# Running sums and new weights of an attention loop, moved from GpSimd to VectorE

## The reference

```python
xn = layernorm(x, g_in)
q = (xn @ Wq).reshape(b, n, H, DH).transpose(0, 2, 1, 3) * scale
kv = xn @ Wkv                       # one key and one value for all heads
sim = einsum('bhid,bjd->bhij', q, k) + bias          # k and v begin with the null key
sim = where(causal or hidden, -max, sim)
attn = softmax(sim, axis=-1)
out = layernorm((attn @ v).reshape(b, n, INNER) @ Wo, g_out)
# second part
xn = out / rms(out) * norm_weight
logits = xn @ router_weight.T + router_bias          # the top 512 tokens of each expert are chosen
y = fc2(gelu(fc1(xn[idx])))                          # 16 experts, 512 -> 2048 -> 512
x = x + (sum of y * gates) / (sum of gates)
```

## Time and profile before

| | |
|---|---|
| median of 3 runs | 2039.32 us (2038.94 to 2042.92) |
| the profiled execution | 2042.92 us, span 2041.2 us |
| busy, share of the span | PE 91%, VectorE (DVE) 75%, ScalarE (ACT) 65%, GpSimd (POOL) 59% |
| granted TensorE clock, mean | 0.961 of full speed |

### The profile page before, as it was taken

The page is one execution under the profiler, slowest core; times in us unless marked ns, Lnnn a source line. Parts: engine busy times, 40 slices in busy tenths (PEclk is TensorE's granted clock), DMA queues, the critical chain, the costliest instruction groups (busy, mean ns, idle before and its releaser), DMA issues.

```text
span 2041.2 us, 41281 instructions
## 1 busy us (share of the span) xinstructions
PE 1861.3 (91%) x12276; PEld 1654.0 (81%) x12276; DVE 1531.3 (75%) x2360; ACT 1321.4 (65%) x2624; POOL 1210.5 (59%) x1224
## 2 busy tenths in 40 slices
PE   2789999986159999999999999999999999999996
PEld 1678888875148898988999889888988999998895
DVE  5678899974886778787777777777777777777763
ACT  3667777762735766666676666666666676766663
POOL 1568888865035646575665657565665756656551
PEclk9899999997559999999999999999999999999998
DMA  5775444432923344353533435254343525434351
GB/s 191 239 207 170 114 120 117 126 98 70 345 63 112 109 133 114 118 139 103 139 108 124 120 123 139 93 142 110 119 124 118 142 90 149 107 125 133 99 130 31
DMA packets 96108, 263.09 MB, mean 129 GB/s; under 512 B 20433, under 2 KB 22193, under 8 KB 93105
## 3 DMA queue, kind: packets, MB, share of 16 engines
q1 hardware_dynamic: 79026, 228.21, 35.1%
q0 software_dynamic: 17024, 34.19, 9.0%
HBM read 223.47 MB, written 55.60 MB: 137 GB/s over the span
## 4 chain that ended last, share of the span: by engine, by line
PE 65%; DVE 4%; ACT 2%; issue 1%; POOL 1%; DMA 0%; DVEq 0%; ACTq 0%; POOLq 0%
PE experts_b_a L2185 17%; PE experts_b_y L273 11%; PE experts_b_y L272 11%; PE experts_b_y L274 11%; PE experts_b_b L2185 9%; PE experts_b_c L2185 4%; ACT experts_h L1697 2%; PE experts_b_turn L2165 1%; DVE experts_x_lo L1851 1%; PE experts_b_turn L2174 1%; PE experts_b_c L2174 1%; DVE experts_w_lo L1911 0%; POOL experts_rows L1521 0%; DVE experts_h_lo L1914 0%; POOL experts_rows_meta L1508 0%
## 5 line engine op out<-in xcount | busy, mean ns | idle before, releaser
L272 PE MATMUL experts_b_y<-experts_w_hi,experts_h_hi 128*128 128x512 f32 x1024 | 406.5, 397 | 0.0
L273 PE MATMUL experts_b_y<-experts_w_lo,experts_h_hi 128*128 128x512 f32 x1024 | 404.6, 395 | 0.0
L274 PE MATMUL experts_b_y<-experts_w_hi,experts_h_lo 128*128 128x512 f32 x1024 | 399.6, 390 | 0.0
L1483 POOL TENSOR_TENSOR experts_s_raw<-experts_w_raw 128x256 f32<-128x256 f32 x128 | 131.9, 1031 | 432.2 <-DMA experts_w_raw<-in_w 431.3
L2185 PE MATMUL experts_b_a<-experts_x_hi,experts_w_hi 128*128 (+1 forms) x1024 | 290.6, 284 | 7.3 <-ACT experts_u_copy L1665 3.2
L2185 PE MATMUL experts_b_a<-experts_x_hi,experts_w_lo 128*128 (+1 forms) x1024 | 290.4, 284 | 0.0
L2185 PE MATMUL experts_b_a<-experts_x_lo,experts_w_hi 128*128 (+1 forms) x1024 | 290.3, 284 | 0.0
L274 PEld LDWEIGHTS experts_b_y<-experts_w_hi,experts_h_lo 128*128 128x128 f32 x1024 | 192.6, 188 | 43.3
L2185 PEld LDWEIGHTS experts_b_a<-experts_x_hi,experts_w_hi 128*128 128x128 f32 x1024 | 195.2, 191 | 27.6 <-issue 6.3
L272 PEld LDWEIGHTS experts_b_y<-experts_w_hi,experts_h_hi 128*128 128x128 f32 x1024 | 194.5, 190 | 24.1
L273 PEld LDWEIGHTS experts_b_y<-experts_w_lo,experts_h_hi 128*128 128x128 f32 x1024 | 194.5, 190 | 21.2
(11 more groups left out here) (366 smaller groups left out, 5489.0 us busy)
## 6 DMA issues: line engine op xcount, KB each, us to landing
experts_w_raw<-in_w SPq DMA_DIRECT2D x256, 512.0 KB
attend_bias<-in_bias SPq DMA_DIRECT2D x68, 256.0 KB, 4.1
attend_spread_w<-weight_dram SPq DMA_DIRECT2D x34, 512.0 KB, 6.5
xn_dram<-g_out_row SPq DMA_DIRECT2D x6, 2304.0 KB, 9.4
attend_q_x<-in_x SPq DMA_DIRECT2D x17, 256.0 KB, 2.9
attend_k_x<-in_x SPq DMA_DIRECT2D x17, 256.0 KB, 5.8
xn_dram<-attend_xn SPq DMA_DIRECT2D x17, 256.0 KB, 4.4
experts_b_sb<-in_b SPq DMA_DIRECT2D x16, 256.0 KB
```

The source lines that it names most:

```text
L272: nc.tensor.matmul(out, lh, rh, start=first, stop=False)
L273: nc.tensor.matmul(out, lh, rl, start=False, stop=False)
L274: return nc.tensor.matmul(out, ll, rh, start=False, stop=last)
L1483: nc.gpsimd.tensor_tensor(s1, a21, a22, ALU.add).then_inc(s_done, 1)
```

## The change

Three operations on 128x16 numbers go from GpSimd to VectorE, and the reciprocal that stood between them joins them in one function `new_sums`. On VectorE the function stands after `key_stats` and before `key_parts`, where before only the reciprocal stood, between `value_parts` and the second `scale_new`. The read of `carry` goes with it. The read of the row number for `keep_logits` moves from ahead of `out_stats` to just ahead of the operation that uses it. Two waits that guarded the hand-over between the engines fall away or change engine.

```diff
--- before.py
+++ after.py
@@ -569,25 +569,6 @@
                     nc.gpsimd.tensor_tensor(state[:, 1, g, :], spread_w[:, 0, g, :], spread_w[:, 1, g, :],
                                             ALU.add).then_inc(o_ready[b], 1)
 
-                def new_sums(n, carry):
-                    done(pool, alpha_ready, n)
-                    free(pool, weight_ready, n)
-                    free(pool, sum_ready, n)
-                    nc.gpsimd.tensor_tensor(kept_sum[:, :], alpha[:, :], flat(total[:, bass.ds(carry, 1), :]), ALU.mult)\
-                        .then_inc(sum_kept, 1)
-                    for c in range(NG):
-                        done(pool, probs_ready[c], n)
-                    free(pool, inv_ready, n)
-                    done(pool, sum_kept, n)
-                    nc.gpsimd.tensor_tensor(total[:, 1, :], kept_sum[:, :], sums[:, :], ALU.add).then_inc(sum_ready, 1)
-
-                def new_weight(n):
-                    new = weight[:, :, :, :].rearrange("p t w g -> p w g t")
-                    done(pool, inv_ready, n)
-                    free(pool, weight_turned, n)
-                    nc.gpsimd.tensor_tensor(new[:, 0, :, :], kept_sum[:, :].rearrange("p (g t) -> p g t", t=2),
-                                            new[:, 1, :, :], ALU.mult).then_inc(weight_ready, 1)
-
                 pool.wait_ge(begun, 1 + CONSTANTS)
 
                 def turn(j, on, upto, edge):
@@ -613,16 +594,10 @@
                         mask_bias(j - 2, 0)
                     if on(-6):
                         out_root(j - 6)
-                    if on(-3):
-                        carry = number(pool, j - 3, 6, 1)
                     if on(0):
                         query_root(j)
-                    if on(-3):
-                        new_sums(j - 3, carry)
                     if on(-6):
                         gain(j - 6)
-                    if on(-3):
-                        new_weight(j - 3)
                     if on(-4):
                         scale_old(j - 4, 0)
                     if on(-2):
@@ -873,12 +848,25 @@
                     g = slice(c * GH, (c + 1) * GH)
                     rest(n, flat(pT_lo[:, g, :]), b_pT[c][:, :], flat(pT_hi[:, g, :]), pT_hi_done[c], pT_done[c])
 
-                def inverse(n):
+                def new_sums(n):
+                    carry = number(dve, n, 6, 1)
                     new = weight[:, :, :, :].rearrange("p t w g -> p w g t")
+                    done(dve, alpha_ready, n)
+                    free(dve, weight_ready, n)
+                    free(dve, sum_ready, n)
+                    nc.vector.tensor_tensor(kept_sum[:, :], alpha[:, :], flat(total[:, bass.ds(carry, 1), :]), ALU.mult)\
+                        .then_inc(sum_kept, 1)
+                    for c in range(NG):
+                        done(dve, probs_ready[c], n)
+                    done(dve, sum_kept, n)
+                    nc.vector.tensor_tensor(total[:, 1, :], kept_sum[:, :], sums[:, :], ALU.add).then_inc(sum_ready, 1)
                     done(dve, sum_ready, n)
                     free(dve, weight_turned, n)
                     nc.vector.reciprocal(new[:, 1, :, :], total[:, 1, :].rearrange("p (g t) -> p g t", t=2))\
                         .then_inc(inv_ready, 1)
+                    done(dve, inv_ready, n)
+                    nc.vector.tensor_tensor(new[:, 0, :, :], kept_sum[:, :].rearrange("p (g t) -> p g t", t=2),
+                                            new[:, 1, :, :], ALU.mult).then_inc(weight_ready, 1)
 
                 def scale_new(n, b):
                     g = slice(b * 4, (b + 1) * 4)
@@ -898,7 +886,8 @@
                     nc.vector.scalar_tensor_tensor(xn[:, :], y[:, :], y_r[:, :], keep["norm_w"][:, :],
                                                    ALU.mult, ALU.mult).then_inc(xn_ready, 1)
 
-                def keep_logits(n, at):
+                def keep_logits(n):
+                    at = number(dve, n, 5, NT)
                     done(dve, logit_ready, n)
                     free(dve, logits_kept, n)
                     nc.vector.tensor_tensor(flat(keep["logits"][:, bass.ds(at, 1), :]), b_lg[:, 0:E],
@@ -948,12 +937,12 @@
                         scale_new(j - 4, 0)
                     if on(-3):
                         value_parts(j - 3)
-                    if on(-3):
-                        inverse(j - 3)
                     if on(-4):
                         scale_new(j - 4, 1)
                     if on(0):
                         key_stats(j)
+                    if on(-3):
+                        new_sums(j - 3)
                     if on(-2):
                         key_parts(j - 2)
                     if on(-3):
@@ -992,12 +981,10 @@
                         query_parts(j - 1, 0)
                     if edge and not on(-4) and on(-5):
                         logits_elsewhere(j - 8)
-                    if on(-7):
-                        at = number(dve, j - 7, 5, NT)
                     if on(-5):
                         out_stats(j - 5)
                     if on(-7):
-                        keep_logits(j - 7, at)
+                        keep_logits(j - 7)
 
                 turns(dve, turn)
```

## The result

The changed kernel takes 2059.93 us (2056.34 to 2061.83, 4 runs) against 2039.16 us: the ratio is 1.0096 (95% interval 1.0077 to 1.0114). That is slower, and above the forecast of 2045.1 and its range, 2036 to 2055. By the medians the change costs 20.8: the profiled execution of the kernel before (2042.92) was the slowest of its four.

A forecast was written before the change was run, and what follows sets the result against it. The prediction took a circle of VectorE waits on GpSimd, above PE's 23.2 us, to set the attention turn. Full turns +9.8, filling -2 and draining -2 gave +5.8 on the median 2039.32: 2045.1 us, range 2036 to 2055.

The forecast's parts named there:

- The ten full turns: Attention loop's full part: every turn becomes 24.57 us instead of a mean 23.59, +9.8 us over ten.
- the exposed read: Register read for the logits, moved behind the output statistics: lies open for 0.45 to 0.5 us a turn.
- the circle from line 551 to `q_mv`: Full turns: VectorE stands behind GpSimd's product of line 551 every turn, then runs to `q_mv`; this sets the turn.
- I cost that at nothing: SP queue: weights, first bias block and query tile about 2 us later, still ahead of use; otherwise up to 1 a turn.
- the filling term of -2: Four filling turns: GpSimd no longer stands behind alpha or the reciprocal; -2 us (-4 to +4).
- Draining: Draining turns: GpSimd's gain and state sums no longer wait for alpha, weights up to 1 later; -2 us (-5 to +2).
- The expert stage at nothing: Routing and expert stage after attention: not touched by the change, forecast 0.
- (1): The forecast itself: every turn locked behind line 551, 2045 us (2041 to 2051), chance 0.50.
- (4): Much slower: lead before line 551's end missed or PE's late scores return; turn 25.3 or more, 2054 us, chance 0.14.
- (5): No visible effect, waits only change places: 2039 us, chance 0.04.
- (3): Faster: VectorE gets both additions out before line 569 every turn; turn 23.3, 2032 us, chance 0.12.
- (2): New operations slip through GpSimd's gaps and fill VectorE's idle 1.02; turn 24.4, 2042 us, chance 0.20.

The follow-up runs named there:

- a_read_back: Changed kernel with the row number for `keep_logits` read ahead of `out_stats` again; 2062.29 us, steady turn 23.93.
- a_one_input: Changed kernel with its three moved operations replaced by one-input reductions, leaving out the running sum; 2054.64 us, steady turn 24.66.
- a_free_max: Changed kernel with the running maximum's two additions and copy replaced by one-input reductions, leaving out the running maximum; 2061.10 us, steady turn 24.51.
- a_carry_early: Changed kernel with the register read of `carry` placed ahead of the key statistics; 2062.44 us, steady turn 24.62.
- a_free_all: Changed kernel with moved operations, running maximum's additions and copy, and line 886's product all made one-input reductions; 2037.56 us, steady turn 23.10.
- a_fill_first: Changed kernel with each filling turn's 2304 KB transfer issued ahead of the weights' transfer in SyncE's list; 2048.50 us.
- a_sums_later: Changed kernel with GpSimd's first weight sums of the expert stage held until VectorE has made the routing keys; 2055.62 us.
- b_fill_first: Kernel before with each filling turn's 2304 KB transfer issued ahead of the weights' transfer in SyncE's list; 2030.19 us.
- b_read_late: Kernel before with only the row-number read for `keep_logits` moved behind `out_stats`; 2043.54 us (ratio 0.9981 to 1.0014).
- b_best: Kernel before with the filling transfer ahead of the weights' and the first weight sums held until the routing keys are made; 2027.06 us.

## Why the prediction was wrong, step by step

- **The ten full turns: right, +10.7 against +9.8.** `v_lo` 1.08 (forecast about 1.0), the three operations held, one turn length of 24.62 to 24.66 (24.57), `kT_lo` 2.8 later (2.9), line 893 (904 before) laid open by its register read. Of the turn the exposed read was mis-sized: 0.71 by a_read_back, where I had taken 0.5. This is 2 us of the total; the rest of the turn was 0.15 shorter than forecast.
- **The reason given for it: half right.** The prediction took the circle from line 551 to `q_mv`. a_one_input agrees with it (waits change places), a_free_max does not. The circle that agrees with all runs is GpSimd's whole run of work from where it takes up `q_mv` to the end of its last mask sum, 18.36, and the rest of VectorE's list until GpSimd takes up the next `q_mv`, 6.28: together 24.64. VectorE can't shorten it by anything that it does ahead of the end of the run as long as it has two-input operations to be held with. a_carry_early, a_read_back and a_free_all each show one side of that.
- **"The queue SP sends the weights, and behind them the first bias block and the query tile, about 2 us later; they land some microseconds ahead of use. I cost that at nothing": this step failed, with the filling term of -2.** It was looked at in the full turns and not in the filling ones, where a transfer of 2304 KB stands between the weights and the bias. There GpSimd and VectorE did wait for landings before the change already (2.40 and 1.60 us), so there was no cover, and 3.4 us of lateness went through in the fourth filling turn, where GpSimd's mask sum came 3.7 later: +5.2 instead of -2, a miss of 7.2 and the largest of all. a_fill_first shows that the loss up to the fifth `v_lo` hangs on this order. It doesn't show that the total miss does: with the order mended in both kernels the change still costs 18.3 by the medians, since the full turns then lose 8.0 more. What makes them do so stays open.
- **Draining: -0.7 against -2.** Within its bounds.
- **The expert stage at nothing: +3.4, of which 2.3 are shown to be wrong.** These stand at the row gather, and a_sums_later takes them away. The change doesn't touch this code; it moves the end of attention against the weights' arrival, and a cast then meets another engine's sum. The remaining 1.1 are smaller than the scatter of the long part.
- The sum of the misses is 7.2 + 0.9 + 1.3 + 3.4 = 12.8; forecast +5.8, measured +18.6 in the trace. The sum was put on the median, which rose by 20.8; the 2.2 between are the spread of single executions.
- The rivals: (1) was right for the turn and wrong for the rest. (4) gave 2054 by a turn of 25.3 or more, which didn't come. (5), no effect, is out by 20 us. (3) and (2) need operations that slip through; in b_fill_first such a state exists for the kernel before, but the changed kernel was never seen in it.

## What to carry to other kernels

A small operation is not free on an engine that another one can hold: ask how many inputs in SBUF it reads and what the other engine runs at that moment, and expect waits to change places until no such operation is left. When a change makes anything later that a queue sends, go through every stretch of the program that issues from that queue, the filling turns above all, and look for a big transfer behind it. Then compare the whole stage and not one mark: what filling won here, the full turns gave back in part. Such neighbours in an order written by hand are worth a look of their own: two such orders gave the kernel before 14 us (2041.33 - 2027.06).

## What was unexpected of the hardware

- Not only two-input operations are held. The prediction had concluded from the reciprocal that operations with fewer inputs in SBUF pass; that was too wide. In b_read_late the copy of line 870, with one input, stood still until GpSimd's sum ended (335.36 and 335.32). The kernel before had this too, 1.23 at 332.12, outside the rows shown:
```profile
334.13 1.23 DVE L870 COPY attend_neg_max<-attend_neg_new 128x16 f32<-128x16 f32 x1
```
```profile
334.03 1.29 POOL L569 TENSOR_TENSOR attend_state<-attend_spread_w 128x512 f32<-128x512 f32 x1
```
The cast above is the second case, while reductions and the reciprocal passed in every trace. The Trainium skill (SBUF — State Buffer, "Who interferes with whom") names copy and cast among the operations that can take the shared port pair, and the reduction among those that never contend on this chip; the traces agree.
- VectorE's cast was held for 2.67 us, over several of GpSimd's operations in a row, not for one: it began at 522.87, in a select of line 1549 that ran until 523.45, and ended at 525.54, when the third sum of 0.71 behind the select did (524.79 + 0.71 = 525.50). The 0.61 in the kernel before is such a select alone (it ends at 508.27, the cast at 508.29).
- The loop of the kernel before ran alternately at 24.6 and 22.8, with the other filling order at 23.09 for six turns and then at 24.84 and 24.63, and with one register read moved at 23.54. b_best, with the same filling order, alternated, so the order doesn't fix it; what does isn't shown.
